# Cross-attention with 20 small heads: units of 256 positions in a loop, against units of 512 positions written out

## The reference, cut to what matters

```python
q = split_heads(x @ Wq.T)                    # 20 heads of 32 channels
k, v = split_heads(text @ Wk.T), split_heads(text @ Wv.T)
k_ip, v_ip = split_heads(ip @ Wk_ip.T), split_heads(ip @ Wv_ip.T)
attend = lambda q, k, v: softmax(q @ k.T / sqrt(32)) @ v
out = merge_heads(attend(q, k, v) + attend(q, k_ip, v_ip))
out = out @ Wo.T + bo + x
```

## Time and profile before

| | |
|---|---|
| median of 3 runs | 683.67 us (683.13 to 684.17) |
| profiled execution: its own time | 683.04 us |
| its span | 681.2 us |
| instructions | 18904 |
| PE busy | 657.5 us (97%) |
| ACT busy | 493.3 us (72%) |
| DVE busy | 435.7 us (64%) |
| POOL busy | 225.0 us (33%) |
| HBM | 67 GB/s over the span |

### The profile page before, as it was taken

One profiled execution on the slowest core, in us unless ns is written; L12 is line 12 of the kernel. 1 busy time (PEld: TensorE's weight loads), 2 busy tenths in 40 slices (PEclk: granted clock), 3 DMA queues, 4 the chain that ended last, 5 costly groups with the idle time before them and its releaser, 6 DMA issues.

```text
span 681.2 us, 18904 instructions
## 1 busy us (share of the span) xinstructions
PE 657.5 (97%) x6514; PEld 564.5 (83%) x6514; DVE 435.7 (64%) x956; ACT 493.3 (72%) x1078; POOL 225.0 (33%) x261
## 2 busy tenths in 40 slices
PE   9959798999999999999999999999999999999997
PEld 9959576788888888888888888888888888888877
DVE  6786677675757566675756576665657566756633
ACT  3983787877868777877777787778777777876730
POOL 4020102243432434343434324343434243342333
PEclk9989898999999999999999999999999999999999
DMA  8950111223131221313131312213131323212212
GB/s 318 410 234 9 25 56 34 80 57 96 49 103 51 82 63 55 93 48 97 51 93 49 99 55 86 55 55 93 48 101 51 90 55 93 56 50 64 56 42 69
DMA packets 34691, 57.46 MB, mean 84 GB/s; under 512 B 4832, under 2 KB 27232, under 8 KB 34400
## 3 DMA queue, kind: packets, MB, share of 16 engines
q1 hardware_dynamic: 34656, 56.99, 27.3%
HBM read 35.34 MB, written 10.49 MB: 67 GB/s over the span
## 4 chain that ended last, share of the span: by engine, by line
PE 85%; DVE 6%; ACT 6%; issue 2%; POOL 0%; DVEq 0%; ACTq 0%
PE q_ps L711 19%; PE x_ps L711 19%; PE sum_ps L769 11%; PE b_ps L752 10%; PE pv_ps L780 10%; PE a_ps L735 7%; PE x_ps L789 5%; PE a_ps L741 1%; ACT probs L405 1%; DVE k_stack L631 1%; DVE k_stack L641 1%; ACT k_stack L485 1%; ACT q_stack L397 1%; DVE wo_lo L554 1%; DVE k_stack L545 1%
## 5 line engine op out<-in xcount | busy, mean ns | idle before, releaser
L405 ACT ACTIVATE probs<-b_ps 77x512 f32<-77x512 f32 x320 | 181.1, 591 | 121.0 <-PE b_ps L752 119.3
L562 DVE TENSOR_TENSOR q_stack<-q_ps,q_hi 32x256 fp32r<-32x256 f32 x320 | 134.3, 420 | 36.0 <-ACT q_hi L390 32.3
L571 DVE TENSOR_REDUCE row_max<-a_ps 128x4 f32<-128x308 f32 x320 | 137.6, 471 | 24.0 <-PE a_ps L735 21.3
L397 ACT ACTIVATE q_stack<-q_hi 32x256 fp32r<-32x256 f32 x320 | 133.0, 416 | 10.0
L598 DVE TENSOR_TENSOR scaled<-x_ps,pv_sb 128x512 f32<-128x512 f32 x75 | 51.9, 692 | 105.4 <-PE x_ps L789 105.0
L752 PE MATMUL b_ps<-q_stack,k_stack 98*77 98x256 f32 x640 | 115.1, 281 | 0.5 <-ACT probs L405 0.5
L347 POOL TENSOR_TENSOR scaled<-scaled 128x256 f32<-128x256 f32 x80 | 59.2, 740 | 139.1 <-DVE scaled L598 139.0
L352 POOL TENSOR_TENSOR attn_lo<-scaled,attn_hi 128x256 fp32r<-128x256 f32 x80 | 59.1, 739 | 113.2 <-ACT attn_hi L434 113.2
L358 POOL TENSOR_TENSOR res<-y,res 128x256 f32<-128x256 f32 x70 | 51.1, 731 | 136.8 <-ACT y L428 136.8
L735 PE MATMUL a_ps<-k_diag,q_hi 128*128 128x308 f32 x320 | 87.3, 313 | 7.0 <-DVE row_max L571 6.8
L752 PEld LDWEIGHTS b_ps<-q_stack,k_stack 98*77 98x77 f32 x640 | 85.7, 146 | 1.5 <-ACT probs L405 1.0
(11 more groups left out here) (111 smaller groups left out, 962.3 us busy)
## 6 DMA issues: line engine op xcount, KB each, us to landing
x_raw<-x_in SPq DMA_DIRECT2D x16, 640.0 KB, 4.2
q_stack<-q_stack SPq DMA_DIRECT2D x80, 128.0 KB, 2.3
res<-x_in SPq DMA_DIRECT2D x75, 128.0 KB, 2.0
y_out<-res SPq DMA_DIRECT2D x75, 128.0 KB, 1.7
stage<-wk_in SPq DMA_DIRECT2D x6, 640.0 KB, 7.9
stage<-wv_in SPq DMA_DIRECT2D x6, 640.0 KB, 10.7
wq_raw<-wq_in SPq DMA_DIRECT2D x1, 1600.0 KB, 10.2
wo_raw<-wo_in SPq DMA_DIRECT2D x1, 1600.0 KB, 14.6
```

The costliest lines, as they stand in the source:

```text
L397: done = nc.scalar.activation(q_stack[0:D, u.slot, j, :], q_hi[j * D:(j + 1) * D, u.slot, :].bitcast(F32), ACT.Copy)
L405: nc.scalar.activation(probs[0:KEYS, j, :], b_ps[j % 2][0:KEYS, :], ACT.Exp).then_inc(b_drained, 1)
L562: done = nc.vector.tensor_tensor(q_stack[D:2 * D, u.slot, j, :], q_ps[rows, 0:N], q_hi[rows, u.slot, :].bitcast(F32), ALU.subtract)
L571: nc.vector.tensor_reduce(row_max[:, u.slot, br, :, sub], bank[:, 0:BLK].rearrange("p (j n) -> p j n", j=GROUP), AXIS.X, ALU.max).then_inc ...
```

## The change: what it does

- A tile is 512 positions (N = 512): 8 tiles, 40 units. q, output, score, sum, value and spread matmuls have 512 columns and are half as many. The maxima keep 308 columns, now eight for a unit, with one transposition of 32 rows.
- The scores of one head and one branch fill a bank (`score_bank`); a unit has eight score matmuls and eight exponentials. pv_ps is two banks.
- There is no x_ps any more. Spreads of the inverse and output chunks borrow the a_ps and b_ps banks (`spread_bank`, `chunk_bank`), so they wait until those are drained, and the next unit's first maxima and scores wait until they are read (`normalised`, `y_done`).
- When they run is a table by the unit's group: `NORM_UNIT` and `CHUNK_UNIT`.
- One slot each of q_hi, row_max, max_rows, x_hi, x_lo; x is split in five chunks. The keys on chip are those of one batch; batch 1's are saved to DRAM at the start and reloaded, group by group, in tile 3.
- DVE adds bias and residual in one instruction from PSUM (`finish`); ACT's `add_bias` and POOL's `add_residual` are gone. The multiply by the inverse is one DVE instruction of 1024 columns, and so is `keep_pv` on ACT. The sum and value matmuls read 77 rows.
- Nothing loops: all 40 units are written out.

```diff
-N = 256
+N = 512
-SPREAD_LAG = 5
-OUT_LAG = 10
+B_ITEMS = GROUP * BRANCHES
+NORM_UNIT = {0: [0], 1: [1, 2], 2: [3, 4]}
+CHUNK_UNIT = {0: [3, 4], 2: [0], 3: [1], 4: [2]}
+def chunk_bank(n):
...
+    return b_ps[:, 0] if m == GROUPS - 1 else a_ps[:, 1]
+def spread_bank(n):
...
+    return b_ps if n % GROUPS in (2, 4) else a_ps
...
 def max_scores(u, k):
     if k == 0:
-        wait(pe, q_hi_done, u.number(1, 1))
-    wait(pe, a_drained, u.number(A_ITEMS, k - 1))
+        wait(pe, q_hi_done, u + 1)
+        wait(pe, normalised, norms_before(u - 1))
...
+    if k == 1:
+        wait(pe, y_done, chunks_before(u - 1))
+    wait(pe, a_drained, u * A_ITEMS + max(k - 1, 0))
...
-def emit(u):
-    find_max(0)
-    find_max(1)
-    scores(u, 0)
-    scores(u, 1)
-    project_q(u.plus(2), 0, 8)
...
+def phase_a(u):
+    max_scores(u + 1, 0)
+    scores(u, 0)
+    max_scores(u + 1, 1)
+    project_q(u + 2, 0, 2)
+    scores(u, 1)
+    for i in range(2, B_ITEMS):
+        max_scores(u + 1, i)
+        project_q(u + 2, 2 * i - 2, 2 * i)
+        scores(u, i)
+    project_q(u + 2, 2 * B_ITEMS - 2, PRODUCT)
+    turn_maxima(u + 1)
+
+for u in range(UNITS):
+    t, g = split(u)
+    phase_a(u)
...
+    if g != 2:
+        for n in chunks_of(u)[:1]:
+            wait(pe, a_drained, min(u + 2, UNITS) * A_ITEMS)
+            project_out(n)
+    if g != 0:
+        for i, n in enumerate(norms_of(u)):
+            if i == 0:
+                wait(pe, a_drained, min(u + 2, UNITS) * A_ITEMS)
+            else:
+                wait(pe, b_drained, (u + 1) * B_ITEMS)
+            spread_inverse(n)
+    row_sums(u)
+    weigh_values(u)
+    if g == 0:
...
+        for n in chunks_of(u)[1:]:
+            project_out(n)
+    elif g == 2:
+        for n in chunks_of(u):
+            wait(pe, a_drained, min(u + 2, UNITS) * A_ITEMS)
+            wait(pe, normalised, n // GROUPS * GROUPS + GROUPS - 1)
+            project_out(n)
...
 # DVE
-    if norm.exists():
-        normalise(norm)
-    if nxt.exists():
-        for k in range(MAXES):
-            max_piece(nxt, k)
-        max_turned(nxt)
-    if u.g == 0 and u.tile_plus(-1).exists():
-        invert_sums(u.tile_plus(-1))
-    if u.plus(2).exists():
-        q_low(u.plus(2))
+    if u + 1 < UNITS:
+        for k in range(MAXES):
+            max_piece(u + 1, k)
+        max_turned(u + 1)
+    if g == 0 and t >= 1:
+        invert_sums(t - 1)
+        for n in chunks_of(u)[:1]:
+            finish(n)
+    if g in (1, 2):
+        for n in norms_of(u):
+            normalise(n)
+    if u + 2 < UNITS:
+        q_low(u + 2)
+    if g == 0:
+        for n in norms_of(u):
+            normalise(n)
+    for n in chunks_of(u)[(1 if g == 0 else 0):]:
+        finish(n)
...
 # ACT, for the group g = 2: x splits and attn_high between the exponentials
+    exp(u, 2); attn_high(back + 2); exp(u, 3); split_x(t + 1, 0); exp(u, 4)
+    keep_pv(u - 1); exp(u, 5); split_x(t + 1, 1); exp(u, 6); exp(u, 7)
+    q_high(u + 2); q_top(u + 2); split_x(t + 1, 2); attn_high(back + 3)
+    split_x(t + 1, 3); attn_high(back + 4); split_x(t + 1, 4)
```

More of the change, by code:

```diff
@@ L234, in stages, with batch_cols, place, x_chunk_free @@
[L234 to L242 removed]
+        def batch_cols(g, b):
+            first = (g // 2 * BATCHES + b) * KEYS
+            return slice(first, first + KEYS)
+        def place(n):
+            t, m = split(n)
+            return t % STEPS, t // STEPS, m
+        def x_chunk_free(eng, t, k):
+            if t >= 1 and k < GROUPS - 1:
+                eng.wait_ge(x_used, (t - 1) * (GROUPS - 1) + k + 1)
+            elif t >= 1:
+                eng.wait_ge(q_acc, t * GROUPS)
@@ L307, in _ @@
[L307 to L315 removed]
+            save_keys()
+            for k in range(GROUPS):
+                load_x(1, k)
@@ L318, in _ @@
+            for n in range(LAST - 3, LAST):
+                store(n)
+                load_residual(n + 2)
+            for m in range(GROUPS):
+                tile, b, _ = place(LAST)
+                sp.wait_ge(last_added, m + 1)
+                sp.dma_start(out_d[tile, b, :, m, :], x_raw[:, m]).then_inc(last_stored, DMA)
+            for s in range(2):
+                sp.wait_ge(stored[s], (LAST + 1 - s) // 2 * DMA)
+            sp.wait_ge(last_stored, GROUPS * DMA)
         @block.gpsimd
@@ L610, in emit @@
[L610 to L623 removed]
+                wait(dve, a_ready, (u + 1) * A_ITEMS)
@@ L836, in grow @@
+            def grow(k):
+                pe.wait_ge(attn_hi_done, LAST + k + 1)
+                chunks = [(bank, slice(m * P, (m + 1) * P)) for m, bank in enumerate(grown)]
+                if k < GROUPS - 1:
                     for out, cols in chunks:
                         for w in (wo_hi, wo_lo):
-                            nc.tensor.matmul(out, w[:, k, cols], attn_hi[:, LAST.batch, k, :],
-                                             start=(k == 0 and w is wo_hi), stop=False, skip_group_check=True)
@@ new lines, in grow @@
+                        nc.tensor.matmul(out, wo_hi[:, k, cols], attn_lo[:, k], start=False, stop=False,
+                                         skip_group_check=True)
+                    return
+                pe.wait_ge(attn_lo_done, LAST + k + 1)
+                for out, cols in chunks:
+                    for w, moving in ((wo_hi, attn_hi), (wo_lo, attn_hi), (wo_hi, attn_lo)):
+                        done = nc.tensor.matmul(out, w[:, k, cols], moving[:, k], start=False, stop=(moving is attn_lo),
+                                                skip_group_check=True)
+                    done.then_inc(out_ready, 1)
```

880 lines of the change are left out of this document (450 added, 430 removed).

## The result

The changed kernel takes **717.97 us** (median of 4 runs, 715.26 to 721.41), the kernel before in the same turns 683.89 us (683.13 to 684.17): ratio 1.0503, 95% interval 1.0444 to 1.0561. The direction was forecast (0.70 for slower); the size was not: the kernel is 34 us slower, where 9 were forecast, and its time lies above the range of 677 to 708. The profiled execution took 715.26 us, the least of the four, with a span of 713.4 us.

The account below looks back on a forecast made before the run. PE bounds the kernel, its saved work set against added waits (7.15 us a tile against 5 x 1.0 saved). Start 67.7, tile 0 59.0, tiles 1 to 7 530.0 and end 34.0 make 690.7 us span, 693 us forecast, range 677 to 708.

Parts of the forecast that it names:

- behind the transposition: In each unit PE waits for the transposition's matmul, DVE's copy and hops: 0.65 us, five times a tile, 3.25.
- behind `finish`: After a chunk last in its unit (groups 0 and 2), PE waits until `finish` has read the bank: 0.75 us, twice.
- q_low, group 1 to 2: PE wants q_low for the next q at 5.9 us, DVE is done at 6.6: 0.75 us a tile.
- eighth score, group 2: The eighth score, due at 6.8 us, waits for ACT's exponentials, attn_hi, x_hi and `keep_pv` until 7.3: 0.75 with restart.
- Rival 3: ACT bounds the units' first halves, exponentials and copies costing 0.1 us more each: 16 us more, 700 to 715, chance 0.15.
- rival 4: Written-out code is slower to fetch, up to 2 us a unit, shown by PE idle under "issue": above 700, chance 0.04.
- that surplus doesn't grow with the columns, so I take 0.2133 + 0.011 = 0.224: PE's 512-column products: the 0.011 us above the columns at 256 and 308 also holds at 512, so 0.224 us each.
- 1.0 us saved by pairs of instructions that become one: PE's work in a new unit: 13.97 us against 14.94 for two old units.
- Rival 2: Every 512-column product, score and spread takes 0.216 us: 12.8 us less, 680 us, range 670 to 682, chance 0.22.
- less 6.7 (tile 1 has no chunks 3 and 4): In the sum for tiles 1 to 7, tile 1's missing output chunks take off 6.7 us.
- the end, 34.0: After the units: inversion, chunk, spreads and five grown chunks with their waits take 34.0 us, before 24.8.
- 1.9 for the last chunk's parts: At the end, PE's wait for the last chunk's parts, 1.9 us, counted within the end's 34.0.

Follow-up runs that it names:

- runs 1, 3 and 6: Changed kernel: chunk waits for its own bank alone, 706.83 us; POOL's end order turned, 712.58; five edits of order together, 689.80, with keep_sums ahead of keep_pv 686.28.
- Run 7: Kernel before with rows of matmuls of several widths and operands appended at its end; 512 columns take 227.0 ns with wo_lo moving, 233.3 with attn_hi.
- Run 2: Changed kernel with every 512-column product split in two of 256, waits and order left: 724.35 us, ratio 1.0600.
- mended kernel: Changed kernel with five edits of order together and keep_sums ahead of keep_pv at the end: 686.28 us, ratio 1.0027.
- Run 3: Changed kernel with POOL's order at the end turned, attn_low ahead of the next add_branches: 712.58 us, ratio 1.0425.
- run 5: Kernel before with its loop over tiles written out, nothing else changed: 685.14 us, ratio 1.0007.

## Why the prediction was right or wrong

**PE's work bounds the kernel, and the waits decide.** Right, and the direction with it. Each place that was named has its wait; by the middle tile of the timeline, over the normal distance:

| place | forecast, a tile | measured |
|---|---|---|
| behind the transposition | 5 x 0.65 = 3.25 | 5 x 0.63 = 3.15 |
| behind `finish` | 2 x 0.75 | 2 x 0.73 |
| q_low, group 1 to 2 | 0.75 | 0.77 |
| eighth score, group 1 | 0.5 | 0.57 |
| eighth score, group 2 | 0.75 | 0.38 |
| other eighth scores, spread | 0.3 + 0.1 | under 0.1 each, not counted |

The measured values hold the restart of 0.10, as the forecast's do. Their sum is 6.3 against 7.15; the difference is mostly the eighth score of group 2, for which the forecast put ACT too late, and the small waits, which did not come. Rival 3 is refuted by the same rows: no eighth score waits in the groups 3, 4 and 0, and the exponentials' mean is 593 ns for 591. The forecast named PE idle under "issue" as the sign of rival 4, and one such wait is there, 3.32 us in tile 1. It does not speak for that rival: it ends 0.10 us behind the multiply that the program waits for there, and it is 3.3 us at the same place in the profiles of the runs 1, 3 and 6.

**The step that failed: "that surplus doesn't grow with the columns, so I take 0.2133 + 0.011 = 0.224".** Two widths, 256 and 308, carried the same surplus in the kernel before, and it was carried over to 512. Measured are 0.232 in the kernel, a surplus of 0.019, and 0.227 at best, 0.013. (Run 7 shows a surplus that stands still with wo_lo moving and one that grows with attn_hi moving; neither is 0.011 at both 256 and 512.) The 0.008 x 1600 are 12.8 us, and the "1.0 us saved by pairs of instructions that become one" is 0.6: a unit costs (78.0 - 6.3) / 5 = 14.34 us, forecast 13.97, before 2 x 7.47. Run 2 shows the price of joining directly. That PE's work sets the pace was right; what failed here is the size of one term. Rival 2, the same number on the other side, was further off. The Trainium skill ("TensorE: Matmul & The Clock Gate", Back-to-back issue gap) gives N/2.4 + 2.5 ns for an isolated warm matmul, 0.216 us for 512; neither the least row (0.227) nor the kernel (0.232) agrees.

**Second: tile 1, "less 6.7 (tile 1 has no chunks 3 and 4)".** The instructions are gone, the time isn't: 77.3 us against 78.0. The chunks were cover for DVE's chain of inversion, q_low and multiply; without them PE waits 1.0 and 3.3 us for it and runs the next matmuls at the lower clock. This is read from the timeline; no run took the chain away. I had costed the removal as pure work and not asked what then stood bare. 6.0 us of the miss. The tile stays that long in the mended kernel too.

**Third: the end, 34.0 against 42.3.** The wait for the inversion was right (3.0 forecast, 2.82 measured). "1.9 for the last chunk's parts" was counted once; POOL's order brings it four times, 1.94 + 1.50 + 1.74 + 1.74 = 6.9, 5.0 more than forecast. 110 products too short by 0.008 add 0.9. The granted clock of the stretch is 0.96, which the sum had no term for; that is at most 0.04 x 42.3 = 1.7 us (an estimate), and 0.7 are left over. Run 3 takes 7.5 us from the last unit and the end together.

**Start and tile 0**: 67.7 and 67.8; 59.0 and 60.9, of which the products are about 1 (five units of 23 x 0.008). The written-out code costs nothing that shows (run 5). Nor does the reload of keys in tile 3, which takes 78.0 us as its neighbours do. The 2.7 us between the profiled execution and the median of 717.97 are of another kind: 0.6 was taken over from the kernel before, but the mean granted clock of the changed kernel's four runs is 0.988, 0.988, 0.981 and 0.979, and the two at the lower clock are the ones of over 720 us (spread 6.2 us; the kernel before 1.0 in its four runs here, up to 3.5 in later ones). Why it differs from run to run is open: run 3, with the same waits in the tiles 0 and 1, spreads 0.6 us.

The misses sum up to +0.1 + 1.9 + 12.4 + 8.3; the 12.4 are 13.0 for the units' work (35 x 0.37), 6.0 for tile 1 and -5.9 for waits (7 x 0.85), 13.1 in sum, 0.7 too many.

## What to carry to other kernels

A price drawn from two neighbouring widths is no price for twice the width: where a change rests on a difference of 10 ns an instruction, bound it by the dearest and the cheapest price per column that the rows allow, and make the whole gain the width of the range. When work goes away, ask what it was covering; the time comes back only if the next engine's chain is shorter than what is left. And when banks are shared, look at the count of each wait: here one that was a step stricter than its own bank needs cost 11 us. Most of what the change lost was never in the tiling: with the order mended the changed kernel comes within 0.3% of the one before, and not under it.

## What was not expected of the hardware

- In rows by themselves a float32r product of 512 columns takes 227 to 237 ns by where its moving rows start in the partition; of 256 columns 113 to 122 were seen. In the kernels the rule did not hold; 40 unused bytes made the kernel before 0.6% slower.
- A float32r product of 128 columns takes 112 ns, hardly less than one of 256 (113 to 122). A float32 matmul of 128 to 512 columns leaves two instructions of 112, 216, 323 and 429 ns each.
- Two kernels that differ only in POOL's order at the end had different clocks in tile 0, behind the same wait of 2.5 us: it took 60.9 us at 1.00 and 63.7 at 0.95.
